# A recurrent block kernel whose opening phase is rearranged: biases whole in fp32, Sign on ScalarE, sums on two engines, four PSUM banks

## The chip, the cores and the metric

The kernel runs on one core of one Trainium2 chip. The metric is the device time of one execution in microseconds. The kernel before takes 267.89 us (median of 3 runs, 267.61 to 268.12).

## What is computed

The input is x, 16 sequences of 128 steps with 128 channels, and everything is fp32. Two layers follow one another:

```python
y   = gelu(x @ W.T + fc_bias + low_rank(x, side) + cond)      # low rank: two small products per sequence, rank 16
Wq  = clip(round(W / (mean(abs(W)) + 1e-5)), -1, 1)           # for W1 and W2: ternary weights
x   = x + relu(y @ Wq1.T + b1) @ Wq2.T + b2
H_t = GRU step(H_{t-1}, x_t)                                  # 128 steps, gates r, z, candidate
Y_t = H_t @ Whq.T + bhq
e   = argmax(Y @ router_w.T + router_b)                       # one of 32 experts per token
x   = x + relu(relu(Y @ w1[e] + b1[e]) @ w2[e] + b2[e])
```

The GRU is sequential. The rest is computed for blocks of steps and is put in the gaps of the recurrence.

## The kernel before

Channels lie on the 128 partitions and tokens in the free dimension. The 128 steps are cut into K = 8 chunks of 16 steps, and a chunk has N = 256 tokens (16 steps by 16 sequences). The main loop runs over chunks k and steps t. Each step is a chain from TensorE to ScalarE (sigmoid), VectorE, TensorE, ScalarE (tanh) and VectorE, with operands split in two fp16 parts (a high and a low one). Around it stand pieces of the feed-forward layer for chunk k + 1 and of the experts for chunk k - 1. The order on each engine is written out by hand, step by step, and engines wait on semaphores.

Before the loop comes an opening phase, which prepares chunk 0 and starts the recurrence:

- Transfers: SyncE issues `ffn_sb` (W1), `second_sb` (low-rank factors, W, and the bias rows `pre_bias_sb`), `gb_sb` (gate biases) and the rest in this order. ScalarE issues `first_sb` (x of chunk 0, low-rank factors and small vectors), W2, and the recurrent weights.
- TensorE (lines 1043 to 1100): `warm_up(24)`, fillers into a bank that nobody reads; two low-rank products for chunk 0; `gamma(0)`, a matmul with ones that adds up the magnitudes of W1 over the partitions; the pre-activation in O (`pre_full`, two `pre_low_rank`, `pre_add_bias`); 6 fillers; `gamma(1)` for W2; 10 fillers; the first half of the hidden layer in fp32 (`first_hidden`, lines 1062 to 1068) with two F banks in turn; three gate biases (`project_bias`); the initial state; low rank for chunk 1; the output layer (`first_out`); and the input projections of step 0 (`project_first`).
- ScalarE (431 to 441): one Erf to load the table, the magnitudes of W2 with an accumulator, the error function of chunk 0, the cast of the recurrent weights to `gru_hi`, four ReLUs (`first_relu`), the cast of the input weights.
- VectorE (668 to 694): magnitudes of W1 (`tensor_reduce`), small copies, masks for the low rank, the thresholds and their negatives, and for W1 and later W2 `below` (a comparison with the negative threshold) and `wq` (above minus below); between the two the gelu of chunk 0; then `gru_lo` and `x1`.
- POOL (284 to 341): constants, then the split in fp16 parts of the bias rows (`pre_rows`, `gbias`), the fp16 copies of `wq` (`wq16`, used from step 6 on), the identity, and the parts of the router's and the experts' biases. SyncE waits for one of them (line 268) and then issues three small transfers.

A bias is added by a matmul: bias rows in fp16, high part in rows from 0 and low part in rows from 32, times a selecting matrix or ones. A matmul in fp32 runs as two pieces, so it stands with x2 in the profile.

In the loop, `w2_high`, `w1_high`, `w2_low` and the low parts of w1 (lines 457 to 488, 696 to 722, 771) prepare the expert weights during chunk 0, and the low parts of the input weights `gru_lo` are made at steps 2 and 3.

Of the kernel before, what the change touches and what calls it, by code (L numbers as in the profile page):

```python
# [55 lines left out]
NV = V_SELECT + B  # L56
WARM_UP, WARM_LATER, WARM_LAST = 24, 6, 10
# [15 lines left out]
def build(nc, xsT, first, second, ffn, gru, gate_bias, consts, expand, router,  # L73
          w1, w2, bias1, bias2, outT):
    ctx = ExitStack()
    with ctx:
# [31 lines left out]
        sizes = sb("sizes", [128, FF])  # L108
# [5 lines left out]
        asum = sb("asum", [128, 2])  # L114
        thr = sb("thr", [128, 2])
        nthr = sb("nthr", [128, 2])
        below = sb("below", [128, 2, FF], F16)
# [99 lines left out]
        pre_rows_made, asum_made, gamma_mm, thr_made, below_made, wq_made = (sem(n) for n in  # L217
            ("pre_rows_made", "asum_made", "gamma_mm", "thr_made", "below_made", "wq_made"))
        gbias_step, b1_step, b1_rows, b2_step, ident_made, expand_made = (sem(n) for n in
            ("gbias_step", "b1_step", "b1_rows", "b2_step", "ident_made", "expand_made"))  # L220
# [64 lines left out]
        def _(pool):  # L285
# [6 lines left out]
            pool.wait_ge(off_set, 1)  # L292
            pool.wait_ge(second_in, 16)
# [51 lines left out]
        def _(act):  # L345
# [11 lines left out]
            def first_relu(half, j):  # L357
                act.wait_ge(first_hid_mm, NF * half + j + 1)
                at = slice(half * 128, half * 128 + 128)
                nc.scalar.activation(hid_first[:, j, at], F_bank[j % 2][:, at], ACT.Relu,  # L360
                                     bias=vec[:, V_B1 + j:V_B1 + j + 1], scale=0.5).then_inc(first_relu_made, 1)
# [71 lines left out]
            act.wait_ge(ffn2_in, 16)  # L433
            nc.scalar.activation(sizes[:], ffn_sb[:, 1, :], ACT.Abs, accum_out=asum[:, 1:2]).then_inc(sizes_made, 1)
            error_function(0)
            act.wait_ge(gru_h_in, 16)
            nc.scalar.copy(gru_hi[:, 0:GATES, :], gru_sb[:, 0:GATES, :]).then_inc(gru_hi_made, 1)
            for j in range(NF):
                first_relu(0, j)
            act.wait_ge(gru_x_in, 16)  # L440
            nc.scalar.copy(gru_hi[:, GATES:WHQ, :], gru_sb[:, GATES:WHQ, :]).then_inc(gru_hi_made, 1)

            for k in range(K):
                par, experts, feed, last = k % 2, k > 0, k < K - 1, k == K - 1
                hidden_at, late = LAST_HIDDEN_AT if last else HIDDEN_AT, FIRST_LATE * (k == 0)
                for t in range(STEPS):
# [13 lines left out]
                    if k == 0 and t in (2, 3, 4, 6):  # L460
                        w2_high((2, 3, 4, 6).index(t))
# [25 lines left out]
                    if k == 0 and t in (2, 4, 5, 6):  # L487
                        w1_high((2, 4, 5, 6).index(t))
# [22 lines left out]
        def _(dve):  # L511
# [132 lines left out]
            nc.vector.memset(asum[:], 0.0).then_inc(warm_set, 1)  # L644
            for tile in (pen, pen_last):
                nc.vector.memset(tile[:], 0.0).then_inc(zeros_set, 1)

            def below_threshold(w, half):
                at = slice(half * 256, half * 256 + 256)
                nc.vector.tensor_scalar(below[:, w, at], ffn_sb[:, w, at], nthr[:, w:w + 1], None,  # L650
                                        ALU.is_lt).then_inc(below_made, 1)
# [8 lines left out]
            def thresholds(w):  # L660
                dve.wait_ge(gamma_mm, w + 1)
                total = R_bank[1][:, N + w:N + w + 1]
                nc.vector.tensor_scalar(nthr[:, w:w + 1], total, -0.5 / (FF * C), -0.5 * EPS,
                                        ALU.mult, ALU.add).then_inc(thr_made, 1)
                nc.vector.tensor_scalar(thr[:, w:w + 1], total, 0.5 / (FF * C), 0.5 * EPS,
# [3 lines left out]
            dve.wait_ge(ffn1_in, 16)  # L669
            nc.vector.tensor_reduce(asum[:, 0:1], ffn_sb[:, 0:1, :], AX.X, ALU.add,  # L670
                                    apply_absolute_value=True).then_inc(asum_made, 1)
# [6 lines left out]
            thresholds(0)  # L678
            dve.wait_ge(thr_made, 2)
            for half in range(2):  # L680
                below_threshold(0, half)
            for half in range(2):
                ternary(0, half)
            twice_gelu(0)
            thresholds(1)
            dve.wait_ge(thr_made, 4)
            for half in range(2):
                below_threshold(1, half)
            for half in range(2):
                ternary(1, half)  # L690
            dve.wait_ge(gru_hi_made, 1)
            nc.vector.tensor_tensor(gru_lo[:, 0:GATES, :], gru_sb[:, 0:GATES, :], gru_hi[:, 0:GATES, :],
                                    ALU.subtract).then_inc(gru_lo_made, 1)
            x1_first(0)

            def first_early(t):
                if t < 2:
                    low_rank_masked(1, t)
                if t in (2, 3):
                    dve.wait_ge(gru_hi_made, 2)  # L700
                    at = slice(GATES * C + (t - 2) * 192, GATES * C + (t - 1) * 192)
                    flat_hi, flat_lo, flat = (w[:].rearrange("p g c -> p (g c)") for w in (gru_hi, gru_lo, gru_sb))
                    nc.vector.tensor_tensor(flat_lo[:, at], flat[:, at], flat_hi[:, at],
# [631 lines left out]
```

## Time and profile before

| | |
|---|---|
| median of 3 runs | 267.89 us (267.61 to 268.12) |
| profiled execution | 267.96 us, of which span 266.2 us |
| mean granted TensorE clock | 0.987 |
| busy | TensorE 239.1, weight loads 174.2, VectorE 225.7, ScalarE 127.7, POOL 15.7 us |
| start of the first recurrent sigmoid | 13.50 us |

The span runs from the first to the last instruction. TensorE's busy time counts fillers too. A matmul's end is modelled and its records overlap, so the chain of waits, where each step begins at the end of what it followed, says more on the pace than the sum of durations.

### The profile page before, as it was taken

The page shows a single profiled execution, that of the slowest core. Times are in us where ns is not written, and L with a number is a line of the kernel's source. Part 1 is how long each engine was busy: PE and PEld are TensorE (multiplying, and loading weights), DVE is VectorE, ACT ScalarE, POOL GpSimd, SP SyncE. Part 2 cuts the span into 40 slices and gives each one's busy share as a digit, 9 for nine tenths or more (in the row PEclk, how much of TensorE's full clock was granted, in tenths as well). Part 3 has the DMA queues.
Part 4 walks back from the last instruction along what each step waited for, and adds up shares of the span by engine and source line. Part 5 has one row for each costly group of instructions (what it writes and reads, how often), then busy time and mean ns, then how long its engine had stood idle before and what let it go on. Part 6 is the DMA issues. An engine that isn't in the chain of part 4 may idle for free.

```text
span 266.2 us, 8917 instructions
## 1 busy us (share of the span) xinstructions
PE 239.1 (90%) x3114; PEld 174.2 (65%) x3114; DVE 225.7 (85%) x1540; ACT 127.7 (48%) x698; POOL 15.7 (6%) x29
## 2 busy tenths in 40 slices
PE   7999889999889998999989998999888888988896
PEld 6887666658665676567665676667665565655586
DVE  3779999998999889988999889989889887788763
ACT  3355654654455444654456444654455444344432
POOL 4872000000000000000000000000000000000000
PEclk9999999999999999999999999999999999999959
DMA  7900000000000000000000000000000000000000
GB/s 253 347 9 4 0 4 2 0 4 0 4 23 0 4 2 20 5 2 0 4 22 0 4 4 18 5 2 0 5 22 1 2 2 1 22 1 4 2 20 22
DMA packets 3372, 5.65 MB, mean 21 GB/s; under 512 B 568, under 2 KB 2128, under 8 KB 3328
## 3 DMA queue, kind: packets, MB, share of 16 engines
q1 hardware_dynamic: 2848, 4.24, 4.5%
q10 hardware_dynamic: 432, 0.74, 0.8%
q8 instruction: 25, 0.41, 0.7%
q14 instruction: 19, 0.16, 0.2%
q0 software_dynamic: 48, 0.10, 0.1%
HBM read 4.03 MB, written 1.05 MB: 19 GB/s over the span
## 4 chain that ended last, share of the span: by engine, by line
PE 49%; DVE 31%; ACT 11%; issue 7%; DMA 1%
PE ZH L971 7%; DVE rh_p L742 7%; PE R L970 7%; ACT R L450 7%; PE R L971 7%; PE ZH L970 6%; DVE m_p L779 6%; DVE zh_p L751 3%; ACT ZH L481 3%; DVE rh_p L747 3%; DVE zh_p L745 2%; DVE rh L743 2%; DVE zh L749 2%; PE F L908 2%; PE L L978 2%
## 5 line engine op out<-in xcount | busy, mean ns | idle before, releaser
L450 ACT ACTIVATE R<-R 128x16 f32<-128x16 f32 x128 | 21.5, 168 | 64.5 <-PE R L971 62.5
L481 ACT ACTIVATE ZH<-ZH 128x16 f32<-128x16 f32 x128 | 21.5, 168 | 55.5 <-PE ZH L971 54.7
L971 PE MATMUL ZH<-rh_p,gru_hi 128*128 128x16 f16 x256 | 44.9, 176 | 0.6
L971 PE MATMUL R<-m_p,gru_hi 128*128 128x16 f16 x254 | 44.6, 176 | 0.0
L971 PE MATMUL ZH<-m_p,gru_hi 128*128 128x16 f16 x254 | 37.4, 169 | 0.0
L970 PEld LDWEIGHTS ZH<-rh_p,gru_lo 128*128 128x128 f16 x128 | 12.3, 96 | 33.8 <-DVE rh_p L742 29.0
L971 PEld LDWEIGHTS ZH<-rh_p,gru_hi 128*128 128x128 f16 x256 | 24.5, 96 | 14.3 <-DVE rh_p L747 0.2
L970 PE MATMUL ZH<-rh_p,gru_lo 128*128 128x16 f16 x128 | 21.7, 169 | 11.3 <-DVE rh_p L742 0.8
L742 DVE TENSOR_TENSOR rh_p<-R,hist 128x16 f16<-128x16 f32 x128 | 22.4, 175 | 9.5 <-ACT R L450 3.2
L779 DVE TENSOR_TENSOR m_p<-keep,ZH 128x16 f16<-128x16 f32 x128 | 21.9, 171 | 9.9 <-ACT ZH L481 8.5
L970 PE MATMUL R<-m_p,gru_lo 128*128 128x16 f16 x127 | 22.9, 181 | 6.2 <-DVE m_p L779 0.2
L1040 PE MATMUL R<-gru_hi 128*128 128x256 f16 x109 | 26.4, 270 | 0.0
L751 DVE TENSOR_TENSOR zh_p<-zh,zh_p 128x16 f16<-128x16 f32 x128 | 22.6, 177 | 4.4
L782 DVE TENSOR_TENSOR m_p<-m,m_p 128x16 f16<-128x16 f32 x128 | 22.4, 175 | 4.3
L971 PEld LDWEIGHTS R<-m_p,gru_hi 128*128 128x128 f16 x254 | 24.6, 97 | 2.0
L971 PE MATMUL ZH<-zh_p,gru_hi 128*128 128x16 f16 x254 | 24.7, 169 | 0.0
L971 PE MATMUL R<-zh_p,gru_hi 128*128 128x16 f16 x254 | 24.7, 169 | 0.0
L454 ACT ACTIVATE keep<-ZH 128x16 f32<-128x16 f32 x128 | 24.6, 192 | 0.0
L971 PEld LDWEIGHTS ZH<-m_p,gru_hi 128*128 128x128 f16 x254 | 24.2, 97 | 0.0
L593 DVE SCALAR_TENSOR_TENSOR hid_lo<-F,hid_hi 128x256 f16<-128x256 f32 x56 | 23.4, 417 | 0.0
L453 ACT ACTIVATE z_sb<-ZH 128x16 f32<-128x16 f32 x128 | 23.0, 179 | 0.3 <-PE ZH L865 0.3
L970 PE MATMUL ZH<-zh_p,gru_lo 128*128 128x16 f16 x127 | 22.9, 181 | 0.0
(249 smaller groups left out, 799.8 us busy)
## 6 DMA issues: line engine op xcount, KB each, us to landing
w_sb<-w SPq DMA_DIRECT2D x2, 512.0 KB, 7.9
outT<-res SPq DMA_DIRECT2D x7, 128.0 KB, 1.9
xs_sb<-xsT SPq DMA_DIRECT2D x1, 640.0 KB, 9.7
first_sb<-first ACTq DMA_DIRECT2D x1, 279.0 KB, 3.6
ffn_sb<-ffn SPq DMA_DIRECT2D x1, 256.0 KB, 3.5
ffn_sb<-ffn ACTq DMA_DIRECT2D x1, 256.0 KB, 4.6
second_sb<-second SPq DMA_DIRECT2D x1, 256.0 KB, 4.2
xs_sb<-xsT SPq DMA_DIRECT2D x1, 256.0 KB, 6.5
```

The costliest lines, as they stand in the source:

```text
L450: nc.scalar.activation(r_io, r_io, ACT.Sigmoid).then_inc(r_made, 1)
L453: nc.scalar.activation(z_sb[:, p, :], z_in, ACT.Sigmoid).then_inc(z_made, 1)
L454: nc.scalar.activation(keep[:, p, :], z_in, ACT.Sigmoid, scale=-1.0).then_inc(keep_made, 1)
L481: nc.scalar.activation(c_io, c_io, ACT.Tanh).then_inc(cand_made, 1)
L593: nc.vector.scalar_tensor_tensor(out=hid_lo[:, c % 4, :], in0=F_bank[c % 2][:, 0:N], scalar=0.0, in1=hid_hi[:, c % 4, :], op0=ALU.max, op1 ...
L742: nc.vector.tensor_tensor(rh_p[:, p, 0, :], r_now, h_old, ALU.mult).then_inc(rh_hi, 1)
L751: nc.vector.tensor_tensor(zh_p[:, q, 1, :], zh[:, q, :], zh_p[:, q, 0, :], ALU.subtract).then_inc(zh_lo, 1)
L779: nc.vector.tensor_tensor(m_p[:, q, 0, :], keep[:, p, :], cand, ALU.mult).then_inc(m_hi, 1)
L782: nc.vector.tensor_tensor(m_p[:, q, 1, :], m[:, q, :], m_p[:, q, 0, :], ALU.subtract).then_inc(m_lo, 1)
L970: mm(out, gru_lo[:, WHR + gate, :], part, start=False, stop=False, skip_group_check=True)
L971: return mm(out, gru_hi[:, WHR + gate, :], part, start=False, stop=low, skip_group_check=True)
L1040: mm(out, gru_hi[:, WHR, :], gru_hi[:, WHZ:WHZ + 2, :], start=False, stop=False, skip_group_check=True)
```

## The change

Eight things are changed, nearly all of them in the opening phase.

1. The biases of chunk 0 are multiplied whole in fp32 (`first_pre_bias`, `first_gate_bias`), with a new selecting matrix at the end of `first_sb` and a tile `top_rows` (ones in rows 0 to 31). The fp16 rows are used from chunk 1 on, and POOL makes them only after the first x1.
2. The magnitudes of each matrix are added by ScalarE (320 of 512 columns for W1, 256 for W2) and VectorE (the rest). `gamma` is two matmuls.
3. The lower comparison is Sign on ScalarE: `side` = sign(w + thr), and `wq` = min(w > thr, side). The negative threshold goes.
4. The first block of the hidden layer has four banks, so it no longer waits for ReLUs.
5. Six fillers go from behind the pre-activation to behind `gamma(0)`, and the last group is 8 instead of 10.
6. The first gate bias comes before the hidden layer, the other two behind it.
7. ScalarE makes `wq16` (steps 2 and 5) instead of POOL.
8. In chunk 0 some casts and low parts are at other steps, and one `w2_low` goes to chunk 1.

```diff
-WARM_UP, WARM_LATER, WARM_LAST = 24, 6, 10
+WARM_UP, WARM_LATER, WARM_LAST = 24, 6, 8
+SUMMED = (320, 256)
...
+        def first_hid_ps(half, j):
+            bank = [F_bank[0], F_bank[1], ZH_bank[1], R_bank[1]][j] if half == 0 else F_bank[j % 2]
+            at = N + 128 if half == 0 and j == 3 else half * 128
+            return bank[:, at:at + 128]
...
             pool.wait_ge(off_set, 1)
+            pool.wait_ge(x1_made, 1)
             pool.wait_ge(second_in, 16)
...
-            for w in range(2):
-                pool.wait_ge(wq_made, 2 * w + 2)
-                t_s(wq16[:, w, :], wq[:, w, :], 0.0, None, ALU.add).then_inc(wq16_made, 1)
-            pool.wait_ge(wq16_made, 2)
...
-            act.wait_ge(ffn2_in, 16)
-            nc.scalar.activation(sizes[:], ffn_sb[:, 1, :], ACT.Abs, accum_out=asum[:, 1:2]).then_inc(sizes_made, 1)
+            def size_sum(w):
+                act.wait_ge((ffn1_in, ffn2_in)[w], 16)
+                nc.scalar.activation(sizes[:, w, 0:SUMMED[w]], ffn_sb[:, w, 0:SUMMED[w]], ACT.Abs,
+                                     accum_out=asum[:, 2 * w:2 * w + 1]).then_inc(sizes_made, 1)
+
+            def side_of(w, half):
+                at = slice(half * 256, half * 256 + 256)
+                act.wait_ge(thr_made, w + 1)
+                nc.scalar.activation(side[:, w, at], ffn_sb[:, w, at], ACT.Sign,
+                                     bias=thr[:, w:w + 1]).then_inc(side_made, 1)
+
+            act.wait_ge(warm_set, 2)
+            size_sum(0)
+            side_of(0, 0)
+            side_of(0, 1)
+            size_sum(1)
             error_function(0)
+            side_of(1, 0)
             act.wait_ge(gru_h_in, 16)
             nc.scalar.copy(gru_hi[:, 0:GATES, :], gru_sb[:, 0:GATES, :]).then_inc(gru_hi_made, 1)
             for j in range(NF):
                 first_relu(0, j)
+                if j == 1:
+                    side_of(1, 1)
...
+            def ternary16(w):
+                act.wait_ge(wq_made, 2 * w + 2)
+                nc.scalar.copy(wq16[:, w, :], wq[:, w, :]).then_inc(wq16_made, 1)
...
-                    if k == 0 and t in (2, 3, 4, 6):
-                        w2_high((2, 3, 4, 6).index(t))
+                    if k == 0 and t == 2:
+                        ternary16(0)
+                    if k == 0 and t in (3, 4, 6, 13):
+                        w2_high((3, 4, 6, 13).index(t))
...
-                    if k == 0 and t in (2, 4, 5, 6):
-                        w1_high((2, 4, 5, 6).index(t))
+                    if k == 0 and t in (2, 4, 6, 15):
+                        w1_high((2, 4, 6, 15).index(t))
+                    if k == 0 and t == 5:
+                        ternary16(1)
...
-                dve.wait_ge(below_made, 2 * w + half + 1)
+                dve.wait_ge(side_made, 2 * w + half + 1)
                 nc.vector.scalar_tensor_tensor(out=wq[:, w, at], in0=ffn_sb[:, w, at], scalar=thr[:, w:w + 1],
-                                               in1=below[:, w, at], op0=ALU.is_gt,
-                                               op1=ALU.subtract).then_inc(wq_made, 1)
+                                               in1=side[:, w, at], op0=ALU.is_gt, op1=ALU.min).then_inc(wq_made, 1)
...
-            thresholds(0)
-            dve.wait_ge(thr_made, 2)
-            for half in range(2):
-                below_threshold(0, half)
-            for half in range(2):
-                ternary(0, half)
+            threshold(0)
+            ternary(0, 0)
+            rest_of_sum(1)
+            ternary(0, 1)
+            threshold(1)
             twice_gelu(0)
-            thresholds(1)
-            dve.wait_ge(thr_made, 4)
-            for half in range(2):
-                below_threshold(1, half)
-            for half in range(2):
-                ternary(1, half)
+            ternary(1, 0)
             dve.wait_ge(gru_hi_made, 1)
             nc.vector.tensor_tensor(gru_lo[:, 0:GATES, :], gru_sb[:, 0:GATES, :], gru_hi[:, 0:GATES, :],
                                     ALU.subtract).then_inc(gru_lo_made, 1)
+            ternary(1, 1)
             x1_first(0)
...
-                if t in (2, 3):
+                if 2 <= t < 5:
                     dve.wait_ge(gru_hi_made, 2)
...
-                if t in (4, 7, 8, 9, 10, 11):
-                    w2_low((4, 7, 8, 9, 10, 11).index(t))
+                if 7 <= t < 12:
+                    w2_low(t - 7)
...
-                    if k == 1 and t in (6, 7):
-                        w2_low(t)
+                    if k == 1 and t in (6, 7, 10):
+                        w2_low((6, 7, 10).index(t) + 5)
...
             def gamma(w):
-                pe.wait_ge((asum_made, sizes_made)[w], 1)
-                mm(R_bank[1][:, N + w:N + w + 1], ones[:], asum[:, w:w + 1], start=True, stop=True).then_inc(gamma_mm, 1)
+                pe.wait_ge(sizes_made, w + 1)
+                pe.wait_ge(asum_made, w + 1)
+                out = R_bank[1][:, N + w:N + w + 1]
+                mm(out, ones[:], asum[:, 2 * w:2 * w + 1], start=True, stop=False)
+                mm(out, ones[:], asum[:, 2 * w + 1:2 * w + 2], start=False, stop=True).then_inc(gamma_mm, 1)
+
+            def first_pre_bias():
+                every = vec[:, V_FIRST:V_FIRST + B].rearrange("p (o b) -> p o b", o=1).broadcast_to([128, STEPS, B])
+                mm(pre_ps(0).rearrange("p (t b) -> p t b", b=B), pre_bias_sb, every, start=False, stop=False,
+                   skip_group_check=True)
+
+            def first_gate_bias(gate):
+                mm(projection(0, gate), gb_sb[:, gate * C:(gate + 1) * C], top_rows[:], start=gate < 2, stop=False,
+                   skip_group_check=True)
...
             gamma(0)
+            warm_up(WARM_LATER)
             pe.wait_ge(second_in, 16)
             pre_full(0, start=True)
+            first_pre_bias()
             pre_low_rank(0, 0)
             pre_low_rank(0, 1)
-            pe.wait_ge(select_made, 1)
-            pe.wait_ge(pre_rows_made, 2)
-            pre_add_bias(0, done=True)
-            warm_up(WARM_LATER)
-            pe.wait_ge(thr_made, 2)
+            pe.wait_ge(thr_made, 1)
             gamma(1)
             warm_up(WARM_LAST)
...
+            pe.wait_ge(gb_in, 16)
+            pe.wait_ge(top_rows_set, 2)
+            first_gate_bias(0)
             pe.wait_ge(g_made, 2)
             first_hidden(0, 0)
             first_hidden(0, 1)
-            pe.wait_ge(gbias_step, 2)
-            for gate in range(GATES):
-                project_bias(0, gate, gate < 2)
             first_hidden(0, 2)
             first_hidden(0, 3)
+            first_gate_bias(1)
+            first_gate_bias(2)
```

## Rows read from the trace of the kernel before

**Rows 1.** Chain of waits, 3 to 9.2 us: start, us, engine, tile, line.
```profile
5.64 0.22 PE R L1000 x2
5.86 1.06 PE O L982 x2
6.92 0.85 PE O L993 x4
7.77 0.21 PE O L986
7.99 0.41 PE ZH L1004 x6
8.40 0.17 PE R L1000 x2
8.57 0.58 PE ZH L1004 x10
```
**Rows 2.** Chain of waits, 9.1 to 15 us.
```profile
9.15 0.56 PE F L1067 x4
9.70 0.11 PE R L860
...
10.03 0.65 PE F L1067 x4
10.68 0.13 PE R L1088 x2
...
11.58 0.91 PE O L1074 x8
...
12.51 0.36 DVE x L520
```
**Rows 3.** Timeline of TensorE, the first fillers: start, us, operation.
```profile
0.97 2.74 PE L1004 MATMUL ZH<-idle 128*128 128x128 f16 x24 [0.97 <-DVE idle L643]
```
**Rows 4.** Timeline of the weight loads, second four of the hidden layer.
```profile
9.94 0.56 PEld L1067 LDWEIGHTS F<-g,wq 128*128 128x128 f32 x4 [0.19 <-ACT hid_first L360]
```
**Rows 5.** Timeline of VectorE.
```profile
4.30 0.69 DVE L670 TENSOR_REDUCE asum<-ffn_sb 128x1 f32<-128x512 f32 x1 [3.09 <-DMA ffn_sb<-ffn]
8.52 0.42 DVE L534 SCALAR_TENSOR_TENSOR g<-erf,O 128x256 f32<-128x256 f32 x1 [0.48 <-ACT erf L390]
10.17 0.87 DVE L656 SCALAR_TENSOR_TENSOR wq<-ffn_sb,thr,below 128x256 f32<-128x256 f32 x2
16.42 0.42 DVE L751 TENSOR_TENSOR zh_p<-zh,zh_p 128x16 f16<-128x16 f32 x1
```
**Rows 6.** Timeline of ScalarE; the last row is tanh of step 2.
```profile
5.77 0.63 ACT L434 ACTIVATE sizes<-ffn_sb 128x512 f32<-128x512 f32 x1 [2.15 <-DMA ffn_sb<-ffn]
8.02 0.38 ACT L390 ACTIVATE erf<-O 128x256 f32<-128x256 f32 x1 [1.53 <-PE O L986]
18.68 0.17 ACT L481 ACTIVATE ZH<-ZH 128x16 f32<-128x16 f32 x1 [0.36 <-PE ZH L971]
```
**Rows 7.** Timeline of POOL.
```profile
6.16 0.42 POOL L296 TENSOR_TENSOR pre_rows<-second_sb,pre_rows 32x128 f16<-32x128 f32 x1
9.50 3.36 POOL L306 TENSOR_SCALAR wq<-wq 128x512 f16<-128x512 f32 x2
21.30 0.81 POOL L341 TENSOR_SCALAR b2part<-b2res 128x128 bf16<-128x128 f32 x1
```
**Rows 8.** Windows of 1 us near the end: busy by engine, granted clock, DMA.
```profile
253.00:254.00 1.00, 0.75 (x14) 0.58 (x15) 0.91 (x8) 0.36 (x4) 0.00 (x0) 0.89 0.00 0
260.00:261.00 1.00, 1.00 (x15) 1.00 (x14) 0.29 (x1) 0.07 (x1) 0.00 (x0) 0.70 0.00 0
```
**Rows 9.** Groups by line, whole span: busy, mean ns, idle before.
```profile
L432 ACT ACT_TABLE_LOAD x1 | 1.3, 1283 | 2.1 <-issue 2.1
L370 ACT ACTIVATE y_hi<-F,first_sb 128x256 f16<-128x256 f32 x7 | 3.3, 473 | 0.4
L751 DVE TENSOR_TENSOR zh_p<-zh,zh_p 128x16 f16<-128x16 f32 x128 | 22.6, 177 | 4.4
```

More of the change, by code:

```diff
@@ L113, in build @@
         ones16 = sb("ones16", [128, N], F16)
[L114 removed]
+        asum = sb("asum", [128, 4])
         thr = sb("thr", [128, 2])
[L116 to L117 removed]
+        side = sb("side", [128, 2, FF], F16)
+        top_rows = sb("top_rows", [128, N])
         wq16 = sb("wq16", [128, 2, FF], F16)
@@ L359, in first_relu @@
                 at = slice(half * 128, half * 128 + 128)
-                nc.scalar.activation(hid_first[:, j, at], F_bank[j % 2][:, at], ACT.Relu,
+                nc.scalar.activation(hid_first[:, j, at], first_hid_ps(half, j), ACT.Relu,
                                      bias=vec[:, V_B1 + j:V_B1 + j + 1], scale=0.5).then_inc(first_relu_made, 1)
@@ L644, in _ @@
             nc.vector.memset(asum[:], 0.0).then_inc(warm_set, 1)
+            nc.vector.memset(top_rows[:], 0.0).then_inc(top_rows_set, 1)
+            dve.wait_ge(top_rows_set, 1)
+            nc.vector.memset(top_rows[0:32, :], 1.0).then_inc(top_rows_set, 1)
             for tile in (pen, pen_last):
                 nc.vector.memset(tile[:], 0.0).then_inc(zeros_set, 1)
[L648 to L651, printed above, removed]
@@ L661, in thresholds, with rest_of_sum, threshold @@
+            def rest_of_sum(w):
+                dve.wait_ge((ffn1_in, ffn2_in)[w], 16)
+                nc.vector.tensor_reduce(asum[:, 2 * w + 1:2 * w + 2], ffn_sb[:, w:w + 1, SUMMED[w]:FF], AX.X, ALU.add,
+                                        apply_absolute_value=True).then_inc(asum_made, 1)
+            def threshold(w):
                 dve.wait_ge(gamma_mm, w + 1)
-                total = R_bank[1][:, N + w:N + w + 1]
-                nc.vector.tensor_scalar(nthr[:, w:w + 1], total, -0.5 / (FF * C), -0.5 * EPS,
-                                        ALU.mult, ALU.add).then_inc(thr_made, 1)
@@ L698, in first_early @@
                     low_rank_masked(1, t)
-                if t in (2, 3):
+                if 2 <= t < 5:
                     dve.wait_ge(gru_hi_made, 2)
-                    at = slice(GATES * C + (t - 2) * 192, GATES * C + (t - 1) * 192)
-                    flat_hi, flat_lo, flat = (w[:].rearrange("p g c -> p (g c)") for w in (gru_hi, gru_lo, gru_sb))
-                    nc.vector.tensor_tensor(flat_lo[:, at], flat[:, at], flat_hi[:, at],
+                    gate = WXR + t - 2
+                    nc.vector.tensor_tensor(gru_lo[:, gate, :], gru_sb[:, gate, :], gru_hi[:, gate, :],
                                             ALU.subtract).then_inc(gru_lo_made, 1)
@@ L1304 @@
             a(L1_cond_bhq)[None]]
+    pick_first = np.where(np.arange(128)[:, None] < 32, pick, f32(0)).astype(f32)
     xsT = a(x).transpose(2, 1, 0).reshape(C, T * B)
@@ L1308 @@
         "first": np.concatenate([xsT[:, 0:N], v.transpose(1, 0, 2).reshape(C, 2 * 128),
-                                 np.concatenate(rows, 0).T, own, pick], 1),
+                                 np.concatenate(rows, 0).T, own, pick, pick_first], 1),
         "second": np.concatenate([v.transpose(0, 2, 1).reshape(2, 128, C), a(L0_cond_W).T[None], twice[None]],
```

48 lines of the change are left out of this document (24 added, 24 removed).

## The prediction

> **What bounds the kernel now.** I read the chain of waits first, in order of time, for the stretch before the recurrence. Between the landing of the first transfer and the first recurrent step it is one engine: TensorE. The chain goes from low rank to gamma, pre-activation, bias, filler, gamma, filler [rows 1], then first hidden layer, gate biases, hidden layer again, carried state and low rank, output layer, and only then VectorE with x1 [rows 2]. Each row starts where the one before it ends; the only hole is in the second group of four hidden records, 0.65 us where the first four took 0.56, of which the view of the weight loads gives 0.19 us to a ReLU [rows 4]. So up to 12.5 us the time is TensorE's queue in its own order, fillers included, and what other engines make ready earlier is worth nothing.
>
> The second thing to see is TensorE's clock. The windows view grants full speed, but the durations show two levels: 24 fillers of 128 columns take 2.74 us, 0.114 each, which is the 1.2 GHz level [rows 3]; the 256-column fp16 bias takes 0.21 us, still 1.2 GHz; six fillers take 0.41 and ten take 0.58 us, 0.058 each, the 2.4 GHz level [rows 1]. The engine had streamed without a gap for over 3 us, and the rise falls at about 8.2 us (1.7 of the six fillers slow, the others fast, make up the 0.41).
>
> Third, the other engines beside it [rows 5 to 7]. POOL has the rows of the pre-activation bias at 6.58 us, over a microsecond before their place in the chain (7.77), and has left the gate-bias rows by 9.50, before theirs (9.70). ScalarE does erf in 8.02 to 8.40, VectorE has g at 8.94, where TensorE leaves its fillers at 9.15. The second ternary matrix is whole at 11.04, the output layer starts at 11.58. None of these waits ends last.
>
> **The change part by part**, on the profiled execution (267.96 us, span 266.2; the median of three runs is 267.89).
>
> Threshold sums. Splitting the magnitudes brings the sum of W1 from 4.99 to between 4.7 and 4.9: the reduce over 192 columns in place of 512 (0.69) is about 0.35, and Abs over 320 about 0.5, by the 0.63 of 512 [rows 5, 6]. But TensorE comes to gamma only near 5.6. Worth 0. The price is that gamma becomes two fp32 matmuls. One costs 0.22, and its second weight load is what makes the 256-column matmul behind it 1.06 and not 0.86, by the 0.85 of two of 128: 0.20 more [rows 1]. So the second pair adds +0.42.
>
> Fillers. Six move from behind the pre-activation to in front of it. There they run at 1.2 GHz, 0.107 each: 0.64 us. The weights that they bridge to have landed by then (TensorE took them up at 5.86 before; now it gets to the fillers at 6.5).
>
> Pre-activation, from 5.64: gamma 0.84, fillers 0.64, matmul 0.86, which makes 7.98. Bias whole in fp32: 0.86 at the slow level instead of 0.21; 0.20 of it passes before 8.18 and the other 0.66 takes half, 0.33: 8.51. Low rank 0.85 slow, 0.43 to 0.46 fast: 8.96. It was 7.99. **+0.97.** The bounds: 1.5 less if the clock were up from 5.2 on, half of 3 us, for the changed kernel alone; 0.3 more if it rises 0.6 later.
>
> From there to the hidden layer. The data path is erf, gelu: 8.02 less 7.99, 0.38, 0.12, 0.42, so 9.91. TensorE's own queue: gamma(1), 0.17 twice, 9.30; eight fillers at 0.058, 9.76; the first gate bias in fp32, half of 0.86, 10.19. The queue ends last, as before (9.15): **+0.07.** Bounds: -0.2, if g decides, to +0.2. The threshold stands ahead of the gelu on VectorE, and follows at 9.35, before erf is done, so it holds up nothing.
>
> Hidden layer in four banks. Eight records, 0.56 and 0.46 without the ReLU's 0.19: 1.02 to 11.21. **-0.19.** Two gate biases in fp32, 0.86 against 0.33 for three in fp16 (9.70 to 10.03) [rows 2]: **+0.53.** Then 10.68 to 12.51 is untouched, 1.83 us, and x1 begins at 13.90. The sum of the parts is 0.97 + 0.07 - 0.19 + 0.53, +1.4.
>
> What has to be ready by 12.97, the new start of the output layer. ScalarE: Sign over 256 columns with a bias from SBUF costs like y_hi's 0.47 [rows 9], four of them; the last stands between ReLU 1 and 2 and ends near 11.6, the last ReLU near 12.2. VectorE has no comparisons of its own any more, and its last ternary piece (0.87 for two before) is done near 12.1. Hidden, 0.8 us to spare; without this cover a Sign costs its 0.4 to 0.47.
>
> POOL now waits for x1 (near 14.3) with the bias rows; its queue holds the pre rows, gate rows, identity, router, and both expert biases. From about 5.5 to 22.1 it took 16.6 us; less the two conversions of wq (3.36) 13.2, so it ends at 27.5 at the latest, and near 26 without its waits for transfers [rows 7]. The first to need it is the bias of block 1 at step 1, near 18, rows ready 15.4; the gate rows are needed at step 5 and ready near 17.8. SyncE's three transfers of the expert-bias rows move by about 4 us and are read in block 1. What I add is that POOL's large operations now lie beside the first steps: one VectorE subtraction there took 0.42 where the mean of its group is 0.18 [rows 5, 9]. 0 to 0.3; I take **+0.1**, less than one such event, since most steps beside POOL show none.
>
> The wq conversions on ScalarE: 512 columns took 0.63 as Abs, against 0.38 of a 256-column erf, the size of the cast that made room: 0.25 more. Step 2 had 0.36 idle before tanh [rows 6], so 0. The conversion in step 5 and the last w1 cast stand behind tanh, where a cast of half the size stood before in steps 2 to 6; bound 0.1. Dividing gru_lo in three, and moving one w2_lo by 22 steps, put 0.28 us where VectorE waits for tanh: 0, bound 0.1 each.
>
> The tail. The granted clock falls to half at 253.9 and is back at 260.7 [rows 8] (a mean of 0.89 over 253 to 254, 0.70 over 260 to 261), over the dense last chunk, whose 128-column records are then the 0.107 ones. If it falls and rises at the same time of the program, a last chunk that comes 1.4 us later has 1.4 us more behind the rise, -0.7, and as much of the thin last steps at half speed, about +0.3. If it goes with the work, 0. I take **-0.3**.
>
> Sum: 1.4 + 0.1 - 0.3 = +1.2, so 269.16 on the profiled execution, 269.1 as a median.
>
> **Rivals.** (A) Sign needs another table. The trace has one table load, 1.28 us, and behind it Erf, Abs, Relu, Sigmoid and Tanh all run [rows 9], but no Sign, so the rows can't exclude it. Place: before the first Sign (its load hides before 9.0) and again before erf: +1.3; before the third Sign, which stands ahead of the ReLUs: +1.3, of which 0.9 is left at the output layer after its slack. 267.96 + 1.2 + 1.3 + 0.2 to 0.9, about 271. The Trainium skill, "ScalarE: Activation LUTs", section "Table sets: the hidden batching unit", names relu, copy, identity and abs as fillers of every set, and Sign isn't in that list. Its section "What ACT_TABLE_LOAD costs" gives about 2.66 us for a switch with its drain; by that the two would cost near 5. 7%.
>
> (B) The other side: the clock doesn't fall in the last steps. TensorE is busy 0.75 of the microsecond of the fall [rows 8], thinner than the steps before, so it stands near whatever decides. Shifted work may miss it. Price: 6.4 us of dense records at half speed, 3.2, less about 0.5 as the last ReLUs and subtractions come to the fore: 267.96 + 1.5 - 2.7 = 266.8. It decides from a shift at which the thin microseconds fall apart in two. Against: four executions within 0.5 us say that this fall comes each time. 12%.
>
> (C) The clock rises some 3 us earlier, since fillers now stand where fp32 weight loads left holes. 3 us of slow work becomes 1.5: 269.1 - 1.5 = 267.6 to 267.9, the same. Against: the holes aren't in the rows, the engine streams in both. 9%.
>
> (D) TensorE's row ends are modelled, and what looks like a full queue is partly waiting for POOL's rows and the ternary values. Then the change takes away real waits (at most 0.5 for the bias and 0.5 for the gates) and gives back most of the 1.4: 268.0. Against: the weight loads are consecutive too. 8%.
>
> **How the numbers follow.** Forecast 64%, its own range 268.4 to 270.2 by the bounds above. 0.2% is 0.54 us, about what a measurement of this kernel can tell. Slower: forecast (62 of its 64) and A, with 2 of D: 0.71. Same: most of C, 4 of D, 2 of the forecast: 0.13. Faster: B, 2 of D, 2 of C: 0.16. The range 267.4 to 270.4 leaves out A and B.
>
> **What would show it.** Right: the erf near 9.0 and x1 near 13.9 where they were 8.0 and 12.5; fillers of 0.107 ahead of the pre-activation; bias matmuls of 0.4 to 0.9; no TensorE wait for POOL. Steps of the recurrence as long as before. Wrong: x1 before 13.0, a second table load, a POOL row as releaser in the first steps, or a tail at full clock.

## The result and the profile after

| | before | after |
|---|---|---|
| median | 268.00 us (4 runs, 267.61 to 268.73) | 272.02 us (4 runs, 270.83 to 273.58) |
| profiled execution, its span | 267.96, 266.2 us | 270.83, 269.0 us |
| mean granted TensorE clock | 0.987 | 0.968 |
| busy TensorE, VectorE, ScalarE, POOL | 239.1, 225.7, 127.7, 15.7 us | 242.1, 225.8, 130.6, 11.9 us |
| start of x1 | 12.51 | 12.24 |
| first `rh_p` of the recurrence (product of R and H) | 13.70 | 13.44 |
| the same operation of the 16th step | 42.84 | 45.36 |
| first 15 steps | 29.14 us | 31.92 us |

The ratio is 1.0147, with a 95% interval of 1.0106 to 1.0189: the kernel is 4.0 us slower, where 1.2 was forecast. The profiled execution is one of the two shorter runs (270.83 and 270.84; the other two took 273.2 and 273.6). It shows where 2.8 us lie, and not where they were expected. The opening came out 0.27 us shorter; the first 15 steps, which were to cost 0.1, cost 2.78; the rest of the span costs 0.28.

The chain of waits of the changed kernel through the opening (start, us, engine, tile, line) answers to [rows 1, 2]:

```profile
4.33 0.49 PE F L997 x2
...
5.04 0.14 PE R L1022 x2
...
5.40 0.36 PE ZH L1036 x6
5.76 0.49 PE O L1001 x2
6.25 0.43 PE O L1027 x2
...
8.66 0.44 PE F L1097 x4
...
9.56 0.87 PE ZH L1031 x4
...
12.24 0.36 DVE x L548
...
13.90 0.52 DVE zh_p L764
...
15.27 0.82 DVE m_p L801
```

TensorE's queue is again one unbroken row, in the order that the prediction wrote down. But the six fillers ahead of the pre-activation take 0.36 us, not 0.64, and the first product takes 0.49 where it took 0.79 before: here the clock is at the 2.4 GHz level from the first product on, in the execution of before it rose at about 8.2. (The granted clock in the windows is 1.00 in both; it is the durations that show the level.) Rival C, then, in this one profile. And behind x1 stand two VectorE rows of 0.52 and 0.82 us which the chain of before doesn't have. The timelines of VectorE and POOL show what lay beside them:

```profile
13.90 0.52 DVE L764 TENSOR_TENSOR zh_p<-z_sb,hist 128x16 f16<-128x16 f32 x1 [0.20 <-ACT z_sb L477]
...
14.98 0.17 DVE L798 TENSOR_TENSOR m_p<-keep,ZH 128x16 f16<-128x16 f32 x1
...
15.27 0.81 DVE L801 TENSOR_TENSOR m_p<-m,m_p 128x16 f16<-128x16 f32 x1
...
13.89 1.17 POOL L307 TENSOR_SCALAR gbias<-gb_sb 128x384 f16<-128x384 f32 x1
15.14 0.90 POOL L309 TENSOR_TENSOR gbias<-gb_sb,gbias 32x384 f16<-32x384 f32 x1
```

The subtraction L801 works on 16 columns and its like take 0.17. It starts 0.13 us into POOL's gate-bias subtraction L309 and ends at 16.08, POOL's ends at 16.04. L764 starts 0.01 after POOL's conversion L307 and takes 0.52. Of about 1 us, the conversion thus makes 0.35 and the subtraction 0.64. These are the bias rows that now wait for x1. Together the two make step 0 3.12 us long, from the first `rh_p` to the second, where before it was 2.14.

The steps behind it aren't held in this way, and are longer all the same: steps 2 to 5 take 2.33, 2.37, 2.59 and 2.20 us where before none took over 1.95. The windows of 1 us show why (busy of TensorE, weight loads, VectorE, ScalarE and POOL, then the granted clock, DMA share and GB/s):

```profile
15.00:16.00 1.00, 0.54 (x12) 0.35 (x9) 0.97 (x4) 0.23 (x1) 0.92 (x2) 1.00 0.06 16
16.00:17.00 1.00, 0.86 (x8) 0.73 (x8) 0.61 (x7) 0.59 (x4) 0.83 (x4) 1.00 0.00 0
17.00:18.00 1.00, 0.95 (x10) 0.85 (x9) 0.93 (x8) 0.44 (x2) 0.83 (x4) 0.84 0.00 0
20.00:21.00 1.00, 1.00 (x18) 0.94 (x16) 0.49 (x4) 0.23 (x4) 0.83 (x3) 0.50 0.00 0
27.00:28.00 1.00, 1.00 (x17) 0.88 (x16) 0.78 (x5) 0.74 (x3) 0.00 (x0) 0.54 0.07 16
256.00:257.00 1.00, 0.74 (x14) 0.48 (x11) 0.94 (x8) 0.34 (x3) 0.00 (x0) 0.81 0.00 0
```

While VectorE was held, TensorE had 0.54 us of work in a microsecond (before it was busy 0.95 to 1.00 in each of the four from 14 to 18 us), and at 17.7 its clock fell to half, the 1.2 GHz level, until 27.9. TensorE is then busy all the time and the recurrence waits for it. The last row is the fall near the end, which comes at about 256.6 in place of 253.8 [rows 8] and lasts to 263.4.

So the theory to test: POOL's two operations on the gate-bias rows hold VectorE in step 0 (about 1 us), the clock falls behind that hole (1 to 1.5 us), and the opening costs its 1.4 us in executions where the clock rises late. The rivals: the longer steps come from the other moves (casts and low parts at other steps), or the fall of the clock would come anyway and is no consequence of the hole.

### The profile page after: what moved, and what is told of

The parts are those of the page before. It is cut to its first block, busy times and chain, and to the rows that moved or that the text cites. A ratio compares the mean times of both kernels' runs of the same rounds, so it can differ in the third digit from the quotient of the medians.

```text
span 269.0 us, 8935 instructions
## 1 busy us (share of the span) xinstructions
PE 242.1 (90%) x3120; PEld 176.8 (66%) x3120; DVE 225.8 (84%) x1538; ACT 130.6 (49%) x706; POOL 11.9 (4%) x27
## 4 chain that ended last, share of the span: by engine, by line
PE 50%; DVE 31%; ACT 10%; issue 6%; DMA 1%
PE ZH L990 7%; PE R L989 7%; DVE rh_p L761 7%; ACT R L474 6%; PE R L990 6%; PE ZH L989 6%; DVE m_p L798 6%; DVE zh_p L770 3%; ACT ZH L507 3%; DVE rh_p L766 3%; DVE zh_p L764 2%; DVE rh L762 2%; DVE zh L768 2%; PE F L927 2%; PE L L997 2%
## 5 line engine op out<-in xcount | busy, mean ns | idle before, releaser
L761 DVE TENSOR_TENSOR rh_p<-R,hist 128x16 f16<-128x16 f32 x128 | 22.3, 174 | 10.6 <-ACT R L474 4.4
L801 DVE TENSOR_TENSOR m_p<-m,m_p 128x16 f16<-128x16 f32 x128 | 23.1, 181 | 4.4
```

The costliest lines, as they stand in the source:

```text
L761: nc.vector.tensor_tensor(rh_p[:, p, 0, :], r_now, h_old, ALU.mult).then_inc(rh_hi, 1)
L801: nc.vector.tensor_tensor(m_p[:, q, 1, :], m[:, q, :], m_p[:, q, 0, :], ALU.subtract).then_inc(m_lo, 1)
```

## The experiments

Every ratio is against runs of the kernel before on the same chip. "15 steps" is the time from the first `rh_p` of the profiled execution to the 16th.

**The change once more, and the kernel before once more.** No edit in either.

> The changed kernel once more, for another profiled execution. If the clock's rise falls at either of two times, it may be the late one here: then x1 begins near 14.3, VectorE stalls by 1.0 us in step 0 all the same, and the time is 271 without and 273 with a fall of the clock behind step 0. If it is the early one: x1 near 12.2, a fall behind step 0, 270.8.

> The kernel before, unchanged, for one more profiled execution and as a measure of the noise. Ratio to itself 1.000, within 0.2%. If the moment at which TensorE's clock rises in the opening phase belongs to the program, it is again near 8.2 us, x1 begins near 12.5 and the loop steps take 31.0 us for the first 16. If that moment differs between executions of one kernel (the changed one rose before 5 us), the rise may be elsewhere, and x1 with it by up to 1.5 us, with no fall of the clock between 13 and 30 us in either case.

The change took 272.44 us in the one run made, span 270.6. This execution shows the other opening; the chain of waits:

```profile
4.73 0.80 PE F L997 x2
...
6.59 0.66 PE ZH L1036 x6
7.26 0.96 PE O L1001 x2
8.22 0.85 PE O L1027 x2
...
10.86 0.44 PE F L1097 x4
...
14.44 0.36 DVE x L548
...
17.46 0.82 DVE m_p L801
```

Fillers, pre-activation and the whole fp32 bias run at the 1.2 GHz level, and x1 starts at 14.44, 1.93 us later than before. 0.31 of that is the first transfer, which let the first product start at 4.73 (before: 4.42). Step 0 takes 3.12 again, the clock is at half from 19.3 to 26.1, and 15 steps take 31.44. The 4.4 us of the span are thus 1.93 of opening, 2.30 of the first 15 steps and 0.17 of all the rest.

The unchanged kernel gave 1.0004 (0.9986 to 1.0022), 15 steps in 29.11, step 0 without a stall: the sum of the 15 steps of before repeats to 0.03 us, a single step to 0.07.

**POOL's rows early again.**

```diff
             pool.wait_ge(off_set, 1)
-            pool.wait_ge(x1_made, 1)
             pool.wait_ge(second_in, 16)
```

> The changed kernel without the wait of POOL for x1: POOL makes the fp16 bias rows from the landing of the weights on, beside the opening phase, as before the change. Theory S (POOL's bias rows beside step 0 stall VectorE by 0.6 and 0.35 us, TensorE runs thin behind it, its granted clock halves for some 10 us and the steps 2 to 5 take 0.3 to 0.7 us longer each): the stall and the fall both go, the first 16 steps take 31.0 us again instead of 33.8, and the time is 2.8 us or more under that of the change, 267 to 269. Theory O (the longer TensorE queue of the opening phase carries the loss, the clock of that one profile hid it): the time stays within 1 us of the change, 270 to 273.

Measured 1.0040 (1.0015 to 1.0065), 269.82 against 268.34 us. The stall is gone (step 0: 2.17), the clock stays up, and 15 steps take 29.22. The medians put what is left of the change at 1.5 us and the wait at 2.5 of the 4.0; the ratios put them at 1.1 and 2.9. The other moves of casts and low parts stand in this kernel and cost nothing that can be seen in its steps. The opening in this profile is the late one, x1 at 14.37. Its 12 times lie in two groups, 268.2 to 268.5 (5) and 269.8 to 270.9 (7). One kernel, two rise times of the clock 4 us apart: that would give such groups, but only one of its executions was profiled, so it is argued. What supports it: this profiled execution (late rise) took 269.81 us and lies in the upper group, and in the kernel with the fillers behind, further down, the profiled one with the early rise took 268.12 and lies in the lower one (268.1 to 268.3, against 269.3 to 270.6). By this reading the rest of the change costs about nothing with the early rise, and 1.9 us with the late one.

**The hole filled.** The stall stays, TensorE gets fillers beside it.

```diff
                         product(z_out, 1, m_p[:, q, 0, :])
+                        if step == 1:
+                            warm_up(10)
                         pe.wait_ge(m_lo, step)
...
                     product(c_out, 2, rh_p[:, q, 0, :])
+                    if step == 0:
+                        warm_up(6)
                     if experts and t in hidden_at:
```

> The changed kernel with 6 fillers on TensorE behind the first candidate product of step 0 and 10 in front of its wait for the low part of m in step 1; POOL's place is as in the change. It takes the clock's part from the stall's. Theory S with the clock: VectorE's stalls of about 1 us in step 0 stay, the granted clock stays full from 14 to 30 us, and 1.5 to 2 us come back: 268.5 to 270.5 with the first 16 steps at 32.0 us. If the stall alone made the loss, nothing comes back: 271 to 273.

Measured 1.0083 (1.0056 to 1.0111). VectorE is held as before (0.52 and 0.81 us), step 0 takes 3.12. The windows beside the two stalls:

```profile
16.00:17.00 1.00, 1.00 (x13) 0.75 (x12) 0.96 (x5) 0.49 (x4) 1.00 (x1) 1.00 0.00 0
17.00:18.00 1.00, 0.97 (x21) 0.86 (x21) 0.97 (x4) 0.31 (x2) 0.92 (x2) 1.00 0.00 0
```

TensorE is busy, the clock doesn't fall up to 30 us, and 15 steps take 30.40, 1.26 more than before. None of the nine profiled executions without a hole of this kind, or with a filled one, has a fall between 13 and 30 us, and all four with an open hole have one. So the fall isn't something that would come anyway: it follows the hole, and costs the difference to 31.44 and 31.92, 1.0 to 1.5 us. Against the change the fillers save 0.6% (1.0083 against 1.0147). Not all of that need be the steps: against the second execution of the change, which has the same opening, this profile is 2.2 us shorter, 1.0 in the first 15 steps and 1.1 behind them, where the last fall is shorter (see the tail, below). And a fall behind step 0 is shown for the profiled executions only: one run of the change took 270.84 us at a mean clock of 0.987, an estimated 7 us at half speed in all, where the profiled one has 17.

**POOL late in the kernel before.** The same four operations once more, behind x1, into a spare tile.

```diff
+            pool.wait_ge(x1_made, 1)
+            t_s(spare_rows[:, 0:C], pre_bias_sb, 0.0, None, ALU.add).then_inc(spare_step, 1)
+            pool.wait_ge(spare_step, 1)
+            t_t(spare_rows[32:64, 0:C], pre_bias_sb[32:64, :], spare_rows[32:64, 0:C], ALU.subtract).then_inc(spare_step, 1)
+            pool.wait_ge(spare_step, 2)
+            t_s(spare_rows[:], gb_sb[:], 0.0, None, ALU.add).then_inc(spare_step, 1)
+            pool.wait_ge(spare_step, 3)
+            t_t(spare_rows[32:64, :], gb_sb[32:64, :], spare_rows[32:64, :], ALU.subtract).then_inc(spare_step, 1)
+            pool.wait_ge(spare_step, 4)
```

> The kernel before with one thing added: after x1 of chunk 0 POOL writes the pre rows and the gate rows once more, into a tile that nobody reads (four operations, 3.0 us), and its later work moves back by as much. The opening phase is that of before. Theory S: VectorE stalls beside these operations in step 0 by up to 1 us, and where TensorE's clock falls after it, 2 us more: ratio to before 1.004 to 1.015. Theory O: 1.000, since the opening phase is untouched.

Measured 1.0052 (1.0032 to 1.0072), step 0 3.10, stalls of 0.50 and 0.81 at the same two lines, clock at half from 17.7 to 24.5, 15 steps 31.41. POOL's four operations reproduce what happened to the steps, with nothing else of the change. The whole costs 1.4 to 1.6 us by ratio and medians, less than the 2.3 of the profiled steps; 270.86 is one of the longer of its runs (268.9 to 271.0). One more thing can be read here. In this execution the clock rose early, and the chain of waits of the opening, which is that of before, is another one:

```profile
1.63 5.78 DMA gb_sb<-gate_bias
...
7.55 1.42 POOL gbias L301
...
9.06 0.91 POOL gbias L303
...
10.02 0.28 PE R L871
...
12.79 0.36 DVE x L531
```

Here TensorE waits for the gate-bias rows from POOL. That is rival D, true in the executions with the early rise: then the kernel before gains nothing from the faster clock (x1 at 12.79 against 12.51), and the changed one does (12.24).

**Which of POOL's operations.** In the kernel before, three of one kind behind x1: first conversions of 128x384, then subtractions of 32x384.

```diff
+            pool.wait_ge(x1_made, 1)
+            t_s(spare_rows[:], gb_sb[:], 0.0, None, ALU.add).then_inc(spare_step, 1)
...
```

> The kernel before with three more tensor_scalar operations on POOL (fp32 to fp16, 128 partitions by 384, 1.2 us each) after the first x1. It asks which of POOL's operations holds VectorE. Theory T (a tensor_tensor on POOL holds the next VectorE operation with two SBUF inputs until it ends): no VectorE operation of the first two steps is over 0.3 us beside them, ratio under 1.002 but for the later place of the rest. Rival (any POOL operation does): an operation of 0.4 to 1.2 us in step 0.

```diff
+            pool.wait_ge(x1_made, 1)
+            t_t(spare_rows[32:64, :], gb_sb[32:64, :], gbias[32:64, :], ALU.subtract).then_inc(spare_step, 1)
...
```

> The same with three tensor_tensor operations on POOL (32 partitions by 384, 0.9 us each) in place of the tensor_scalar ones. Theory T: one or more VectorE operations of up to 0.9 us in steps 0 and 1, each ending with a POOL operation; step 0 and 1 together 1 to 2 us longer, and a fall of the clock behind them in some executions: ratio 1.004 to 1.012. Rival: as with tensor_scalar.

The conversions: 1.0000 (0.9981 to 1.0018), 15 steps 29.62. One VectorE operation was held, in the timelines:

```profile
15.13 0.48 DVE L758 TENSOR_TENSOR zh<-z_sb,hist 128x16 f32<-128x16 f32 x1
...
15.05 1.19 POOL L314 TENSOR_SCALAR spare_rows<-gb_sb 128x384 f16<-128x384 f32 x1
```

It ends at 15.61, 0.56 us after the conversion began and 0.63 before that ended. The expectation, that a conversion holds nothing for over 0.3 us, didn't come true. That the conversions cost no time isn't settled: the ratio shows none, but its interval leaves room for 0.5 us, and 0.48 is what the 15 steps of this profile took more than before. The clock stayed up.

The subtractions: 1.0054 (1.0036 to 1.0072), step 0 3.25, 15 steps 31.34.

```profile
14.50 0.77 DVE L754 TENSOR_TENSOR zh_p<-z_sb,hist 128x16 f16<-128x16 f32 x1 [0.21 <-ACT z_sb L462]
...
15.47 0.77 DVE L760 TENSOR_TENSOR zh_p<-zh,zh_p 128x16 f16<-128x16 f32 x1
...
14.33 0.90 POOL L314 TENSOR_TENSOR spare_rows<-gb_sb,gbias 32x384 f16<-32x384 f32 x1
15.31 0.90 POOL L316 TENSOR_TENSOR spare_rows<-gb_sb,gbias 32x384 f16<-32x384 f32 x1
...
14.04 0.17 DVE L751 TENSOR_TENSOR rh_p<-R,hist 128x16 f16<-128x16 f32 x1 [0.84 <-ACT R L459]
```

Other VectorE lines than in the change, and each again ends 0.03 to 0.04 us after the POOL subtraction that it fell into. The length is set by what is left of POOL's operation, not by the line. The last row shows one that wasn't held: it lies within POOL's first subtraction (13.35 to 14.26), but takes one of its operands from PSUM (R), where the held ones take both from SBUF. The clock was at half from 22.3 to 25.7.

**Fillers back behind the pre-activation** (with POOL early).

```diff
             gamma(0)
-            warm_up(WARM_LATER)
             pe.wait_ge(second_in, 16)
...
             pre_low_rank(0, 1)
+            warm_up(WARM_LATER)
             pe.wait_ge(thr_made, 1)
```

> The changed kernel with POOL early (as in the second run), and the six fillers behind the pre-activation again. Prices the fillers' place. Where the clock rises only at 8 us (late): six fillers took 0.66 us of the queue in front, so x1 begins 0.4 to 0.65 earlier than the 14.37 of the second run, near 13.8. Where it rises before 5 (early): at most 0.2, since the queue is short there. Median 0.3 to 0.5 under the second run's 269.8. Rival: the fillers filled a real wait, and x1 stays within 0.1.

Measured 1.0043 (1.0017 to 1.0069), beside the 1.0040 of the kernel with POOL early: no gain, where 0.3 to 0.5 us was expected. Its profile has the early rise (x1 at 12.63, the first product 0.24 later than in the change, so 0.15 worse), and so can't show the price of the fillers at the slow level. That stays open.

**Biases in fp16 rows again** (with POOL early).

```diff
             pre_full(0, start=True)
-            first_pre_bias()
             pre_low_rank(0, 0)
             pre_low_rank(0, 1)
+            pe.wait_ge(select_made, 1)
+            pe.wait_ge(pre_rows_made, 2)
+            pre_add_bias(0, done=True)
...
-            first_gate_bias(0)
...
+            for gate in range(GATES):
+                project_bias(0, gate, gate < 2)
...
-            first_gate_bias(1)
-            first_gate_bias(2)
```

> As the second run, with the biases of chunk 0 in fp16 from POOL at their old places (pre-activation last, three gate biases between the hidden products), fillers in front, two gamma matmuls, four banks. Prices the fp32 biases. Late clock: 0.65 less for the pre-activation and 0.5 less for the gates, so x1 begins near 13.2 instead of 14.37. Early clock: TensorE comes to the gate biases near 9 and waits for POOL's rows until 9.9, so x1 begins near 12.7 and nothing is gained over the 12.24 of the change. If the fp32 biases cost nothing in either, x1 stays at 14.37 and 12.24.

Measured 1.0023 (1.0001 to 1.0045), x1 at 13.64 with the late rise, where the kernel with POOL early has 14.37. That is 0.7 us of x1, and 0.5 us of the median (+0.97 against +1.48 us over before), though the intervals of the two ratios overlap, so that only x1 shows it clearly. It was to be 13.2: the chain now goes through gelu (g at 9.85, 0.43) and the hidden layer starts at 10.33 behind it, since the erf comes behind fillers at the slow level. The data path is the wait that took over from the queue.

**The parts put together.** Sign on ScalarE and four banks from the change; one gamma per matrix, fillers behind, fp16 bias rows and POOL early as before; the output layer ahead of the gate biases.

```diff
+            for j in range(NF):
+                first_hidden(0, j)
...
+            for j in range(NF):
+                first_out(0, j)
+            pe.wait_ge(gbias_step, 2)
+            for gate in range(GATES):
+                project_bias(0, gate, gate < 2)
```

> What should beat both: Sign on ScalarE and four banks from the change; one gamma matmul each, fillers behind the pre-activation, the fp16 biases and POOL's place from the kernel before; new is the order behind the hidden layer: low rank, output layer, and only then the gate biases and the initial state, beside VectorE's x1 (0.5 us in which TensorE had idled). Late clock: x1 near 11.6 instead of 12.5, the first step 0.9 us earlier. Early clock: POOL's rows at 9.9 bind nothing any more, x1 near 11. Ratio 0.995 to 0.998. Rival: the ReLUs or the second ternary matrix come last, and x1 is not under 12.2; ratio 0.999 to 1.001.

Measured 0.9978 (0.9957 to 0.9999), x1 at 12.53, no earlier than before. So the opening isn't where this profile gains: what follows the 16th step is 1.0 us shorter than before. The chain of waits:

```profile
9.22 0.51 ACT side L442
9.73 0.40 ACT gru_hi L453
10.13 0.61 ACT hid_first L362 x2
10.74 0.40 ACT side L442
...
11.17 0.50 DVE wq L677
...
11.80 0.68 PE O L1097 x4
```

Once TensorE's queue is shorter, the last Sign on ScalarE decides, with the cast of the recurrent weights and two ReLUs ahead of it. So, against the kernel just described:

```diff
             side_of(1, 0)
-            act.wait_ge(gru_h_in, 16)
-            nc.scalar.copy(gru_hi[:, 0:GATES, :], gru_sb[:, 0:GATES, :]).then_inc(gru_hi_made, 1)
+            side_of(1, 1)
             for j in range(NF):
                 first_relu(0, j)
-                if j == 1:
-                    side_of(1, 1)
+            act.wait_ge(gru_h_in, 16)
+            nc.scalar.copy(gru_hi[:, 0:GATES, :], gru_sb[:, 0:GATES, :]).then_inc(gru_hi_made, 1)
...
-            warm_up(WARM_LATER)
             pe.wait_ge(thr_made, 1)
             gamma(1)
-            warm_up(WARM_LAST)
+            warm_up(WARM_LATER + WARM_LAST)
```

and on VectorE both ternary pieces and x1 before `gru_lo`.

> The seventh run had its output layer wait for the second ternary matrix (11.67 us), whose Signs stood between other work of ScalarE and whose gamma stood behind six fillers. Here gamma(1) comes right behind the pre-activation, both Signs of W2 before the ReLUs, and the cast of the recurrent weights and its low part behind them. Late clock: the hidden layer starts near 9.2, the output layer near 10.8, x1 near 11.7 instead of 12.53, 0.7 to 0.9 us off the time: ratio 0.993 to 0.996. Rival: the cast moved behind the ReLUs comes last (gru_lo, before the first step), and x1 moves but the first step doesn't: ratio 0.997 to 0.999.

Measured 0.9925 (0.9901 to 0.9949), 266.95 against 268.70 us: faster than both kernels. The chain has no wait for another engine left between the landing and the output layer:

```profile
8.31 0.39 PE R L1013 x2
8.69 0.80 PE ZH L1026 x14
9.50 0.53 PE F L1088 x4
...
10.47 0.45 PE L L991 x4
10.92 0.89 PE O L1095 x8
```

x1 starts at 11.85, and the output layer, at 10.92, stands 0.66 us earlier than in [rows 2], since nothing that only the recurrence needs is ahead of it.

But the opening is only part of the gain. The profiled span is 1.6 us shorter than that of before: 0.66 by x1, nothing by the 15 steps (29.16 against 29.14), and 0.97 behind the 16th step, where the last fall of the clock lasts 3.4 us instead of 6.8:

```profile
254.00:255.00 1.00, 0.78 (x10) 0.52 (x10) 0.77 (x6) 0.66 (x3) 0.00 (x0) 0.65 0.37 131
257.00:258.00 1.00, 1.00 (x15) 1.00 (x13) 0.93 (x5) 0.04 (x1) 0.00 (x0) 0.65 0.00 0
```

No experiment shows that the order of the opening brought this about.

## Why the prediction was wrong

The sign was right, the size was not: 269.1 was forecast and 272.0 measured, outside the range.

**The step that failed is POOL's.** "0 to 0.3; I take **+0.1**, less than one such event, since most steps beside POOL show none." Measured: +1.0 in step 0 (3.12 against 2.14), and 2.3 to 2.8 over 15 steps with what it brought about. The row for it was there [rows 5]: 0.42 us of a subtraction at 16.42. I took about its excess over the mean as the bound of such an event, as if that were a size of its own. What it shows is that it ended with POOL's own subtraction, which in the trace of before runs from 16.39 to 16.81:

```profile
16.39 0.42 POOL L323 TENSOR_TENSOR b1res<-b_sb,b1part 8x128 f32<-8x128 f32 x1
```

The question was how long the moved operations are. The gate-bias subtraction takes 0.9, so a hold could be as long as that, and was 0.81. And "most steps show none" doesn't bound it: whether a step shows one depends on whether a VectorE operation with two SBUF operands falls into a subtraction of POOL, or into the first half of a conversion (0.35 more here). The subtractions cost most: 15 steps take 31.34 with three of them, 29.62 with three conversions and 29.14 with neither.

The Trainium skill says this outright: "SBUF — State Buffer", section "SBUF: two separate sides", calls the pair of ports that VectorE and GpSimd share an exclusive lock, which whichever of a VectorE operation with two SBUF inputs and a GpSimd operation starts first keeps for its whole instruction. For subtractions the traces agree (0.81, 0.77 and 0.77 us, ended with POOL's). For the conversions they don't: VectorE was let go 0.53 to 0.56 us into operations of 1.2 us.

**The clock was costed in the opening and in the tail, and not between.** The prediction says that TensorE "stands near whatever decides" in the last steps, and asks nothing of the kind of step 0, where a held VectorE leaves TensorE with 0.54 us of work in a microsecond. The fall behind it was put at nothing. The kernel with fillers in the hole prices it: 1.0 to 1.5 us.

**The opening: with the late rise the mechanism was right, the size a little small.** +1.4 was forecast for x1. With the early rise x1 came 0.27 earlier than before, and the term doesn't hold. The execution with the late rise gives +1.93, or +1.62 without the later landing. By the terms, from gamma on: the stretch to the end of low rank was to be 3.32 us and took 3.61, since the whole bias passed at the slow level (0.85 instead of 0.53; the named bound "0.3 more if it rises 0.6 later"). From there to the hidden layer 1.30 against 1.23, the eight hidden records 0.89 against 1.02 (four banks, better than forecast), two gate biases 0.87 against 0.86, and the rest 1.82 against 1.83. In medians the kernel without the wait is 1.5 us slower than before, close to the forecast, which is +1.1 without POOL's term; but those medians mix both rises, so the closeness is in part luck.

**The tail** was put at -0.3. What follows the 16th step differs from before by +0.28 in the profiled execution of the change and by +0.17 in the second one; the fall went with the work here, the case priced at 0. But in the kernel with fillers and in that with late subtractions the same stretch is 0.89 and 0.84 us shorter, with a fall of 3.4 us near 258 in place of 6.8; so it is in the two put-together kernels (1.0 us shorter, falls of 3.4 us at about 254.5). In all 13 profiled executions this stretch is 223.1 to 223.6 us with a last fall of 6.8, and 222.3 to 222.5 with one of 3.4. So the sum has a term of up to 1 us that no edit here controls.

**Hidden costs.** Threshold sums, VectorE's comparisons, the casts in the steps: 0, as forecast; with POOL early 15 steps take 0.08 us more than before. The Sign pieces on ScalarE were hidden too (0.4 to 0.5 us each, the 0.47 of [rows 9]); they came to the fore only in the shorter opening above.

**The rivals.** A didn't come: there is one table load in the whole span, with Sign behind it; the group by line of the changed kernel:

```profile
L435 ACT ACT_TABLE_LOAD x1 | 1.3, 1283 | 2.1 <-issue 2.1
```

B didn't come in the change: the fall at 256.6 is in the windows. Its reason doesn't hold either: in the trace of before the microseconds from 250 and from 252 us were thinner (0.72 busy), and the clock stayed full in both. C came in one of two profiles of the change: it took 0.27 off where +1.4 stood, about what its 1.5 us said, and was buried under the steps. D is true, but only with an early rise.

## What to carry to other kernels

Work moved off the opening to an idle engine is not free if that engine shares something with the bound one: before moving a POOL operation beside a latency chain, look in the trace for VectorE operations longer than their group's mean, and compare their end with POOL's. Where they end together, a moved operation can cost up to its own length, once for each operation of the chain that falls into one. Then ask what stands idle during that stall, and what TensorE's clock does behind it; and when a queue is shortened, look at once for the engine that comes to the fore.

## What the runs showed of the hardware

- A POOL subtraction of 32x384 (0.90 us) held a VectorE operation of 16 columns for 0.77 to 0.81 us instead of 0.17, to within 0.04 us of its own end, in each of the five executions that had one beside the first step. The held ones had both operands in SBUF; one with an operand in PSUM took its 0.17 us beside such a subtraction. A POOL conversion of 128x384 (1.17 to 1.19 us) let a held VectorE operation go 0.53 to 0.56 us after its own start; one that began 0.71 us into a conversion wasn't held (0.17 us).
- In four executions the clock fell to half behind a few thin microseconds of TensorE (0.72, 0.54 and 0.86 busy in the change), in three at once and in the one with late subtractions only at 22.3 us, and stayed down for 10.2, 6.8, 6.8 and 3.4 us, though TensorE was busy for 0.95 to 1.00 of each full microsecond in that time. Thin microseconds alone don't tell a fall: beside x1 TensorE was busy 0.46 of the one from 12 us in the change, and the clock stayed up.
- The first rise of the clock, read from the durations, differs between executions: it had come by the first product at 4.3 to 4.8 us, which took 0.49 us (the first execution of the change, the kernel before with POOL late, the one with fillers behind), or it came at about 8 to 9.7, and the first product took 0.79 to 0.80 (all others). The 24 fillers ahead were at the 1.2 GHz level in both (2.74 us). The landing of the first transfer doesn't decide it: with 3.56 and 3.81 us the rise was early, with 3.65 and 3.96 late. What does stays open. A change of an opening has to be costed at both.
